# The first half of a mixture-of-experts routing and one normalisation, moved from inside a scan to behind it

## The reference

```
dA = exp(d_i[..., None] * A)
h = dA * h + (d_i * u_i)[..., None] * B_i[:, None, :]
y = einsum('bdn,bn->bd', h, C_i)
```

```
scores = sigmoid(xf @ gate_w.T); s = scores + gate_bias
... 2 groups with the largest maximum, then the top 4 experts in them
y = sum over chosen experts of comb[t, e] * (silu(x w1_e) * (x w3_e)) w2_e
```

## Time and profile before

| | us |
|---|---|
| median of 3 runs (lowest, highest) | 1132.51 (1130.37, 1134.35) |
| the profiled execution | 1132.16 |
| its span, first to last instruction | 1130.1 |
| TensorE clock granted, mean over the span | 0.933 of full |
| PE busy | 935.6 (83%) |
| DVE busy | 834.2 (74%) |
| POOL busy | 645.7 (57%) |
| ACT busy | 622.3 (55%) |
| first scan instruction starts | 784.68 |
| last product with C by DVE ends (1013.46 + 1.21) | 1014.67 |

### The profile page before, as it was taken

How to read it: one execution, slowest core, us unless ns; L and a number is a source line. 1 busy time by engine, 2 the same in 40 slices (tenths; PEclk the granted TensorE clock), 3 DMA queues, 4 the chain that set the end, 5 groups by cost and what they waited for, 6 DMA issues and landing times.

```text
span 1130.1 us, 11134 instructions
## 1 busy us (share of the span) xinstructions
PE 935.6 (83%) x2933; PEld 543.9 (48%) x2933; DVE 834.2 (74%) x1175; ACT 622.3 (55%) x1131; POOL 645.7 (57%) x445
## 2 busy tenths in 40 slices
PE   6869975788889957999999999865678787586997
PEld 3324432233347635788888888421223232134775
DVE  4995437999955578566666666577999999963754
ACT  5756676301366653566555555767555565334556
POOL 3030135699741224677777777303999999642773
PEclk9979998799999958999999999988898999888999
DMA  2000120000020004676766766002323233240251
GB/s 80 1 0 1 49 75 17 0 0 1 0 69 1 14 15 98 146 155 137 160 149 142 159 140 155 0 1 65 87 85 84 71 79 81 65 124 18 60 149 38
DMA packets 29928, 78.25 MB, mean 69 GB/s; under 512 B 3968, under 2 KB 13824, under 8 KB 25696
## 3 DMA queue, kind: packets, MB, share of 16 engines
q1 hardware_dynamic: 29888, 77.78, 27.7%
HBM read 75.93 MB, written 1.84 MB: 69 GB/s over the span
## 4 chain that ended last, share of the span: by engine, by line
PE 36%; DVE 16%; ACT 4%; issue 4%; POOL 1%; DVEq 0%; ACTq 0%
PE ps L605 36%; DVE y L3053 4%; DVE g L3053 4%; DVE tmp L2371 2%; DVE g L3009 1%; ACT ps L1389 1%; ACT sq L1389 1%; DVE rstd L2371 1%; DVE g L2371 1%; ACT g L1389 1%; DVE ps L2371 1%; DVE arena L2371 1%; ACT rstd L1389 0%; DVE resid L2371 0%; ACT arena L1389 0%
## 5 line engine op out<-in xcount | busy, mean ns | idle before, releaser
L605 PE MATMUL ps<-parts 128*128 128x512 f32 x1704 | 416.2, 403 | 18.8 <-DVE g L2371 6.2
L605 PEld LDWEIGHTS ps<-parts 128*128 128x128 f32 x1704 | 321.6, 190 | 108.0 <-issue 17.9
L605 PE MATMUL ps<-g,arena 128*128 128x512 f32 (+2 forms) x408 | 197.1, 622 | 36.1 <-POOL g L2274 15.1
L1389 ACT ACTIVATE g<-ps 128x512 f32<-128x512 f32 (+1 forms) x216 | 127.2, 597 | 148.2 <-PE ps L605 142.1
L2371 DVE TENSOR_TENSOR ps<-g,ps 128x512 f32<-128x512 f32 x160 | 111.3, 696 | 94.6 <-PE ps L605 73.2
L2328 POOL TENSOR_TENSOR g<-g 128x1024 f32<-128x1024 f32 x64 | 149.1, 2362 | 54.3 <-DVE g L2371 54.3
L2225 POOL TENSOR_TENSOR parts<-g,parts 128x512 fp32r<-128x512 f32 x112 | 144.5, 1291 | 59.5 <-ACT parts L1389 56.6
L605 PEld LDWEIGHTS ps<-g,arena 128*128 128x128 f32 (+1 forms) x408 | 78.5, 201 | 146.9 <-issue 90.3
L1389 ACT ACTIVATE ps<-g,small 128x512 f32<-128x512 f32 x131 | 89.3, 687 | 98.8 <-DVE y L3053 51.3
L1389 ACT ACTIVATE parts<-g 128x512 fp32r<-128x512 f32 (+3 forms) x243 | 125.8, 546 | 25.1 <-DVE g L2371 17.8
L2371 DVE TENSOR_TENSOR g<-ps,g 128x512 f32<-128x512 f32 (+1 forms) x140 | 98.9, 707 | 20.1 <-PE ps L605 3.9
(11 more groups left out here) (223 smaller groups left out, 1164.0 us busy)
## 6 DMA issues: line engine op xcount, KB each, us to landing
g<-coef_scratch SPq DMA_DIRECT2D x56, 512.0 KB, 6.2
g<-b_scratch SPq DMA_DIRECT2D x64, 256.0 KB, 3.3
g<-in_moe_dram SPq DMA_DIRECT2D x34, 192.0 KB, 4.7
g<-coef_scratch SPq DMA_DIRECT2D x24, 256.0 KB, 5.0
arena<-coef_scratch SPq DMA_DIRECT2D x24, 256.0 KB, 4.1
g<-in_rope_dram SPq DMA_DIRECT2D x1, 2048.0 KB, 8.8
g<-in_moe_dram SPq DMA_DIRECT2D x2, 768.0 KB, 7.4
arena<-in_weights_dram SPq DMA_DIRECT2D x1, 1348.5 KB, 6.0
```

Of the source, the lines that this page charges most:

```text
L605: return nc.tensor.matmul(o, lhsT, rhs, start=start, stop=stop, **kw)
L1389: return nc.scalar.activation(o, i, func, **kw)
```

## The change

On DVE, `h_back7(2)`, `clip7(2)` and the routing of half 0 leave the loop for places behind it; PE's `router7(2)` and `coef_turned7(0)` and `(1)` and ACT's `coef_copied7(0)` and `(1)` leave it too. `pre7_var(2)` and `pre7_root(2)` move from states 13 and 15 to 10 and 12. Rows 0 to 47 of B go to another part of SBUF; the first four are loaded after the first of four stores. POOL's first product waits for `dl_ready` and no longer for the last `du_ready`.

```diff
         def b_copy(step):
-            return g[:, 8, step % 4 * N:(step % 4 + 1) * N]
+            home = arena[0][:, 1792:3840] if step < 48 else g[:, 8, :]
+            return home[:, step % 4 * N:(step % 4 + 1) * N]
@@ SP, layer 6
-                    for c in range(CHUNKS):
+                    def store_b(c):
                         sp.wait_ge(s["b_copied"], c + 1)
                         sp.dma_start(b_dram[:, cols(c)], b_rows[:, cols(c)]).then_inc(s["b_stored"], 16)
+                    store_b(0)
+                    sp.wait_ge(s["b_stored"], 16)
                     for step in range(STEPS):
                         k = step % 4
-                        if step < 4:
-                            sp.wait_ge(s["dl_ready"], step + 1)
-                        else:
+                        if step == 4:
+                            for c in range(1, CHUNKS):
+                                store_b(c)
+                        if step == 16:
+                            sp.wait_ge(s["b_stored"], 16 * CHUNKS)
+                        if step == 48:
+                            sp.wait_ge(s["dl_ready"], CHUNKS)
+                        if step >= 4:
                             sp.wait_ge(s["db_ready"], step - 3)
-                        if step == 0:
-                            sp.wait_ge(s["b_stored"], 16 * CHUNKS)
@@ PE
             def post6_var(c):
-                if c:
+                if 0 < c < 3:
                     pe.wait_ge(s["sc_clipped"], 2 + c)
             def pre7_var(c):
-                if c == 2:
-                    pe.wait_ge(s["ct_ready"], CHUNKS + 1)
             def coef_turned7(c):
-                bank = {0: variance7(0), 1: centred7(1), 2: ps[:, 2, :], 3: ps[:, 3, :]}[c]
+                bank = ps[:, c, :]
                 pe.wait_ge(s["coef_ready"], 3 + c // 2)
-                if c == 0:
-                    pe.wait_ge(s["rstd_ready"], post6_count(NORM["post6"], 2))
-                if c == 1:
-                    pe.wait_ge(s["x_ready"], x_at(7) + 3)
-                if c > 1:
+                if c < 2:
+                    pe.wait_ge(s["yg_ready"], CHUNKS)
+                else:
                     pe.wait_ge(s["sc_clipped"], 6)
-            for step in range(STEPS + 3):
+            for step in range(STEPS):
-                if step >= 3:
+                if 3 <= step < STEPS:
                     sum_n(step - 3)
+                if step == STEPS - 1:
+                    sum_n(step - 2)
-                    if n == (10, 10, 13)[c]:
+                    if n == 10:
                         pre7_var(c)
-                    if n == (13, 13, 15)[c]:
+                    if n == 13 and c < 2:
                         router7(c)
-                if step == 58:
-                    coef_turned7(0)
-                    coef_turned7(1)
             def gate_up7(n):
                 if n == 0:
-                    pe.wait_ge(s["ct_ready"], CHUNKS + 2)
+                    pe.wait_ge(s["x_ready"], x_at(7) + 3)
             def down7(n):
-                if n == 0:
-                    pe.wait_ge(s["yg_ready"], CHUNKS)
-                if r == 0 and c >= 2:
-                    pe.wait_ge(s["ct_ready"], 2 * CHUNKS)
+                if r == 0:
+                    pe.wait_ge(s["ct_ready"], CHUNKS + 2 * (c // 2 + 1))
+            sum_n(STEPS - 2)
+            sum_n(STEPS - 1)
+            router7(2)
             gate_up7(0)
             out_of(3)
             gate_up7(1)
             post6_var(3)
             pre7_var(3)
+            coef_turned7(0)
+            coef_turned7(1)
             router7(3)
@@ ACT
-                    if n == (12, 12, 15)[c]:
+                    if n == 12:
                         pre7_root(c)
                 if step == 60:
-                    coef_copied7(0)
-                    coef_copied7(1)
                     weights7_hi(0)
...
             pre7_root(3)
+            coef_copied7(0)
+            coef_copied7(1)
             sigmoid7(1)
@@ POOL
-                    pool.wait_ge(s["du_ready"], CHUNKS)
+                    pool.wait_ge(s["dl_ready"], CHUNKS)
                     def b_times_du(step):
+                        if step % 16 == 0:
+                            pool.wait_ge(s["du_ready"], step // 16 + 1)
@@ DVE
-                    if n == (12, 12, 14)[c]:
+                    if n == 12 and c < 2:
                         h_back7(c)
-                    if n == (14, 14, 15)[c]:
+                    if n == 14 and c < 2:
                         clip7(c)
-                if k == 53:
-                    group_scores7(0)
-                if k == 54:
-                    group_order7(0)
-                if k == 55:
-                    kept7(0)
-                if k == 57:
-                    chosen7(0)
...
+            h_back7(2)
             gate(CHUNKS - 1)
+            clip7(2)
+            group_scores7(0)
+            group_order7(0)
+            kept7(0)
             add_back6(3)
+            chosen7(0)
             h_back7(3)
             clip7(3)
```

More of the change, by code:

```diff
@@ L1993, in coef_copied7 @@
             def coef_copied7(c):
-                bank = {0: variance7(0), 1: centred7(1), 2: ps[:, 2, :], 3: ps[:, 3, :]}[c]
                 act.wait_ge(s["ct_bank"], CHUNKS + c + 1)
-                f(coef_rows7[:, cols(c)], bank[0:16, :], ACT.Copy).then_inc(s["ct_ready"], 1)
+                f(coef_rows7[:, cols(c)], ps[0:16, c, :], ACT.Copy).then_inc(s["ct_ready"], 1)
             def weights7_hi(r):
```

## The result

The changed kernel takes 1119.07 us (median of 4 runs, 1112.98 to 1121.23) where the kernel before takes 1132.03 on the same chip: ratio 0.9875, interval 0.9831 to 0.9920. A second measurement with more runs gives 1117.85 against 1132.60: 0.9855, interval 0.9826 to 0.9884. 1116.4 was forecast, a ratio of 0.9858 to 1132.5.

What follows compares the result with a forecast made beforehand. DVE was taken to bound the scan, stretched and held up by PE and ACT in the last chunk, PE the tail. Gains 15.94 + 0.2 = 16.1 from 1132.16 give 1116.1, plus 0.35 for the median 1116.4; range 1112.4 to 1121.2.

Steps and rivals of the forecast that it cites:

- The loop: Scan 52 to scan 63: 51.13 us before, 35.19 forecast from the same stretch of the chunk before, a gain of 15.94.
- DVE idle ahead of scan 61 for ACT: Late in the scan loop: listed as a sign that the prediction is wrong; no size given.
- From the last product of C to `out_of(3)`: 0: Tail behind the scan: PE is busy without a break and makes the same work in another order, so 0 gained.
- The rival of the tail on DVE: Tail hangs on DVE's last product, not on PE: gain 18.6 us, time 1113.9; chance 0.10.
- The ladder at 0: Small steps behind the scan: the moved routing fits ahead of `add_back6(3)` with 2 us to spare, cost 0.
- The rival of the routing on the ladder: Behind the scan: the moved routing delays `router7(3)`, costing 2 to 5 us, time 1118.4 to 1121.4; chance 0.20.
- Coefficients at 0: Their later copies, store and load still reach `glu7(2)` in time, with 1.8 us of cover: cost 0.
- Weights at 0: First experts' weights, loaded behind B's last row: 1.9 us left for ACT, cost 0, up to 1.5 if slower.
- The start at 0.2: Scan start: POOL's first product may begin sooner but waits DVE out; 0.2 us gained, between 0 and 1.25.
- Clock rival: Expert stage runs long at 1.2 GHz on PE; a quarter of the stage gives 1139.9 us; chance 0.03.
- The sum: Whole kernel: 15.94 for the loop plus 0.2 for the start, 16.1 us gained.

Runs made afterwards that it cites:

- weights_early: Changed kernel with the loads of the first experts' weights issued before the row of B for step 63, not after it: 1116.65 us, ratio 0.9857 to before.
- ladder_root: Changed kernel with PE's order of ladder and `pre7_root(2)` one step later on ACT: 1115.56 us, ratio 0.9874 to before.
- norm_stays: Changed kernel with chunk 2's norm, router and clip back at their old places in the scan, routing still behind it: 1122.57 us, ratio 0.9903 to before.
- pool_beside_order: Changed kernel with two unread products added on POOL beside `group_order7(0)`: 1117.98 us, ratio 0.9861 to before.
- du3_late: Changed kernel with DVE's last product of delta*u issued behind the first two scan instructions, not ahead of them: 1120.19 us, ratio 0.9878 to before.
- slack: Changed kernel with router, rounding and `h_back7` of chunks 0 and 1 one step later and their clip in the next chunk: 1118.47 us, ratio 0.9897 to before.
- best: Changed kernel with the edits of slack and ladder and the later `pre7_root(2)` together: 1111.13 us, ratio 0.9822 to before.
- ladder: Changed kernel with `out_of(3)` and `post6_var(3)` ahead of both `gate_up7` on PE behind the sums: 1116.08 us, ratio 0.9854 to before.

## Why the prediction was right

**The loop** was forecast at 15.94 and gave 15.36 against the same profile that the forecast was read from. The method, the same stretch of the chunk before less what that chunk has more, was right, and the term is off by 0.58: the subtraction took `h_back7(1)` out at 0.60 as if it cost what it lasts. It covered ACT's root and rounding, and without it DVE waits 0.56 us at scan 61. The prediction named the place (DVE idle ahead of scan 61 for ACT) and gave it to a late load of weights; weights_early refutes that, ladder_root shows the root. The idle time there was one of its own signs of being wrong, and it came. A second fault doesn't show in this number: the 1.89 us of DVE's wait for PE were taken as a fixed part of the loop. They are 1.89, 1.13 and nothing in three profiles of that code, and where they lack, the ladder is longer. The sum of loop and ladder, 15.3 to 15.7 us against a forecast of 15.94, is what the runs bear out. The order's 6.02 us were read as 1.5 each and are three stretched operations and a short one, which changes nothing in the sum.

**From the last product of C to `out_of(3)`: 0** is right. `out_of(3)` follows scan 63 by 12.99 us, by 13.09 before, and norm_stays shows that 3.00 us of DVE's waiting buy 0.1. The rival of the tail on DVE falls.

**The ladder at 0** is right for the routing's part, by the row that was chosen: the order took 1.15 us for an estimated 1.2. `add_back6(3)` waits 3.04 us where "2 us to spare" was said. The rival of the routing on the ladder falls here by idle POOL, and pool_beside_order shows what it rested on: with POOL at work nearly all the room is gone. That the whole stretch came out at 29.20 and 29.21 is luck: it takes 30.16 and 31.85 in the two other profiles of the old code, by where PE's clock was low.

**Coefficients at 0**: right. Their rows land at 1020.10 and DVE reads them at 1021.70, behind a wait for PE; 1.6 us of cover, 1.8 were estimated. **Weights at 0**: right. The first load landed 1.2 us ahead of its rounding, where 1.9 were left by estimate.

**The start at 0.2** is right in size (0.22 by DVE's wait ahead of scan 0) and mechanism: POOL's first product took 3.38 us, so it stood still while DVE finished, and du3_late gives the rest back when the partner is moved. The value itself was chosen between two bounds and not worked out.

**Clock rival**: the last chunk's clock rose from 0.86 to 1.00 and the experts ran no longer than before (93.39 and 94.13), so the slower side did not come.

**The sum** by the profiles is 15.36 + 0.2, and 0 for the rest, plus 0.7 to 1.5 in the experts that nobody forecast: 16.3 to 17. That this meets 16.1 so closely is in part luck, as the loop's 0.58 too little and the experts' unforecast gain stand against each other. The comparisons give 14.1 us (0.9875) and 16.4 (0.9855), with intervals of 5 us to either side in the first and 3.3 in the second. That the median lies above 1116.4 fits the 3.5 us of the scan's two long steps, which several of the profiles have. Whether they are a term of the change stays open.

## What to carry to other kernels

Price an operation at the place where it will stand, by a row of its kind taken while the other engines do what they will do there: here the same four operations cost 6.02, 4.11 or 1.15 us, by what POOL does beside them. When an instruction is taken off the engine that bounds, ask what it covered on the others: its duration is the gain only if nobody is late behind it, and the second half of its step (here the root on ACT) should move with it. ladder_root shows it for one place, slack for two more. And compare kernels by stretches cut at common landmarks, since a whole time mixes the change with stretches that vary by themselves, but take more than one profile of each: here two neighbouring stretches of the same code moved by 2.4 and 2.7 us, and their sum by 0.3.

## What was not expected of the hardware

**The same exclusion moves the expert stage by 1.5 us.** That stage, the same code in all, took 93.2 to 93.5 us in eight profiles, 94.1 in before and best, and 95.0 in four. The order of the other half's groups (`group_order7(1)`) stands at its beginning, on DVE beside POOL's rounding. DVE and then POOL in slack (94.96):

```profile
1025.69 1.15 DVE L2377 TENSOR_TENSOR tmp<-tmp 128x128 f32<-128x128 f32 x2
1026.87 1.37 DVE L2377 TENSOR_TENSOR tmp<-tmp,arena 128x128 f32<-128x128 f32 x1
1028.28 0.99 DVE L2377 TENSOR_TENSOR tmp<-tmp 128x128 f32<-128x128 f32 x1
```

```profile
1025.19 1.30 POOL L2219 TENSOR_TENSOR parts<-g,parts 128x512 fp32r<-128x512 f32 x1 [0.22 <-ACT parts L1394]
1026.80 1.29 POOL L2219 TENSOR_TENSOR parts<-g,parts 128x512 fp32r<-128x512 f32 x1 [0.31 <-ACT parts L1394]
```

and in the kernel after (93.39):

```profile
1024.50 0.48 DVE L2377 TENSOR_TENSOR tmp<-tmp 128x128 f32<-128x128 f32 x2
1025.02 0.29 DVE L2377 TENSOR_TENSOR tmp<-tmp,arena 128x128 f32<-128x128 f32 x1
1025.34 0.29 DVE L2377 TENSOR_TENSOR tmp<-tmp 128x128 f32<-128x128 f32 x1
```

```profile
1023.21 1.29 POOL L2219 TENSOR_TENSOR parts<-g,parts 128x512 fp32r<-128x512 f32 x1 [0.32 <-ACT parts L1394]
1025.69 1.29 POOL L2219 TENSOR_TENSOR parts<-g,parts 128x512 fp32r<-128x512 f32 x1 [1.19 <-ACT parts L1394]
```

In slack three of the four operations meet one of POOL's and last as long as that has left, 3.5 us for the four (the second, 0.28 us, falls between two of them); in the kernel after they fall into POOL's hole from 1024.50 to 1025.69 and take 1.1. The hole goes with a slower PE: its granted clock was 0.50 behind the silu in both, and at or near full from the sixth us on in the kernel after, from the fourth in slack, and POOL's next rounding waited 1.19 us. All profiles fit: the four operations span 1.1 us in the six stages of 93.4 to 93.5, 1.2 and 1.5 in the two of 93.2, 2.7 in before and best, 3.6 in the four of 95.0. In ladder, whose clock rose in the fifth us, they span 1.5 and the stage is the shortest, so a slower PE helps only as far as it takes POOL out of DVE's way. This is read from the profiles; no run set the phase by itself.

**A drop of TensorE's clock costs engines that aren't TensorE.** The 1.8 us on DVE at each of two steps of the scan are larger than any wait that the change left in the loop. The stretch ahead of the store of B, the same code in all profiles, took from 751.46 to 757.25 us, and the time it spent at the lower clock went from 80 to 95 us in the same order but for small exchanges; that the clock makes the difference there is likely by this, but no run shows it. Between the two profiles of the changed kernel, 8.7 of the 8.9 us of difference lie in these two stretches.
